# Spreading a weight quantisation over three engines in an attention and feed-forward kernel, with GpSimd taking q's parts ahead of k's

## The reference

```python
xn = layernorm(x)
# attention: 16 query heads and 4 key/value heads, 8 features each, causal
q = rope((xn @ Wqa @ Wqb).reshape(b, s, 16, 8))
k, v = split((xn @ Wkva @ Wkvb).reshape(b, s, 4, 8, 2)); k = rope(k)
attn = softmax(causal(q @ k.T * 8 ** -0.5)) @ v @ Wout + bout
# feed-forward, fp4 linear: both operands are quantised and dequantised
def fp4_quant_dequant(x):          # per block of 16
    scale = max(max(abs(xb)) / 6, 1e-12)
    return grid(abs(xb / scale)) * sign(xb) * scale
gate, up = fp4_linear(xn, w_gate), fp4_linear(xn, w_up)      # 128 -> 352
ffn = fp4_linear(silu(gate) * up, w_down)                    # 352 -> 128
out = x + attn + ffn
```

## Time and profile before

| | us |
|---|---|
| median of 3 runs | 919.4 |
| lowest, highest | 917.61, 923.97 |
| the profiled execution: time | 914.5 |
| the profiled execution: span of the core | 912.7 |
| TensorE busy | 765.5 (84%) |
| VectorE, GpSimd, ScalarE busy | 643.7, 593.8, 568.4 |
| mean granted TensorE clock | 0.989 |

### The profile page before, as it was taken

The page is one execution under the profiler, slowest core; times in us unless marked ns, Lnnn a source line. Parts: engine busy times, 40 slices in busy tenths (PEclk is TensorE's granted clock), DMA queues, the critical chain, the costliest instruction groups (busy, mean ns, idle before and its releaser), DMA issues.

```text
span 912.7 us, 22388 instructions
## 1 busy us (share of the span) xinstructions
PE 765.5 (84%) x6769; PEld 486.9 (53%) x6861; DVE 643.7 (71%) x1444; ACT 568.4 (62%) x1201; POOL 593.8 (65%) x688
## 2 busy tenths in 40 slices
PE   2376889898997989879897989979988998988786
PEld 1233555656564565646555565645656565655443
DVE  4789877787776877666776778758786877677501
ACT  1134677666757766665765667567666768576673
POOL 3446777678766767667676677656677777765541
PEclk9998999999999999989999999999999999999999
DMA  5314121323232122322312132221223222130000
GB/s 132 94 33 114 55 62 41 89 62 90 53 84 69 53 60 54 90 53 71 74 59 62 52 89 63 82 60 49 64 54 89 64 86 55 53 77 12 25 23 13
DMA packets 66279, 58.47 MB, mean 64 GB/s; under 512 B 17299, under 2 KB 56179, under 8 KB 66171
## 3 DMA queue, kind: packets, MB, share of 16 engines
q1 hardware_dynamic: 66170, 57.04, 23.4%
HBM read 31.81 MB, written 18.61 MB: 55 GB/s over the span
## 4 chain that ended last, share of the span: by engine, by line
PE 45%; ACT 15%; issue 15%; DVE 11%; POOL 6%; another core or an unknown queue 3%; SPq 2%; DMA 1%; DVEq 0%; ACTq 0%; POOLq 0%
PE pv_ps L1033 10%; PE exp_ps L1015 7%; ACT P L836 6%; PE max_ps L1000 5%; DVE neg_max L641 5%; PE misc_ps L1100 5%; PE misc_ps L1051 4%; POOL P L491 3%; PE misc_ps L1061 3%; PE max_ps L1001 2%; PE misc_ps L1069 2%; ACT oT L855 2%; ACT h_mag L946 2%; PE misc_ps L1098 2%
## 5 line engine op out<-in xcount | busy, mean ns | idle before, releaser
L641 DVE TENSOR_REDUCE neg_max<-max_ps 128x1 f32<-128x512 f32 (+3 forms) x768 | 430.9, 597 | 180.2 <-PE max_ps L1001 177.9
L836 ACT ACTIVATE P<-exp_ps 128x512 f32<-128x512 f32 x512 | 293.1, 604 | 197.7 <-PE exp_ps L1015 106.4
L1015 PE MATMUL exp_ps<-Q,K 128*128 128x128 bf16 (+3 forms) x932 | 210.8, 294 | 26.6 <-ACT P L836 22.6
L1000 PE MATMUL max_ps<-K,Q 128*128 128x384 bf16 (+2 forms) x768 | 198.9, 278 | 37.8 <-DVE neg_max L641 15.9
L1001 PE MATMUL max_ps<-Kd,Q 128*128 128x128 bf16 x1024 | 190.5, 221 | 1.0 <-DVE neg_max L641 0.8
L1033 PE MATMUL pv_ps<-P,V 128*32 128x512 f32 (+3 forms) x2048 | 165.3, 438 | 5.9 <-issue 2.6
L491 POOL TENSOR_SCALAR_AFFINE_SELECT P<-P 128x512 f32<-128x512 f32 x256 | 154.0, 638 | 19.2 <-ACT P L839 19.2
L1000 PEld LDWEIGHTS max_ps<-K,Q 128*128 128x128 bf16 x768 | 76.4, 100 | 112.3 <-DVE neg_max L641 47.7
L1001 PEld LDWEIGHTS max_ps<-Kd,Q 128*128 128x128 bf16 x1024 | 100.4, 99 | 36.9 <-issue 18.6
L1015 PEld LDWEIGHTS exp_ps<-Q,K 128*128 128x128 bf16 x1024 | 79.6, 98 | 71.9 <-ACT P L836 46.6
L839 ACT ACTIVATE P<-exp_ps 128x512 f32<-128x512 f32 x128 | 78.3, 612 | 36.8 <-PE exp_ps L1015 36.7
(11 more groups left out here) (112 smaller groups left out, 1084.1 us busy)
## 6 DMA issues: line engine op xcount, KB each, us to landing
Q<-q_scr SPq DMA_DIRECT2D x64, 224.0 KB
q_scr<-q_split SPq DMA_DIRECT2D x16, 384.0 KB, 2.6
Kd<-K SPq DMA_DIRECT2D x64, 96.0 KB
x_in<-x SPq DMA_DIRECT2D x16, 256.0 KB, 2.8
q_scr<-q_split SPq DMA_DIRECT2D x16, 256.0 KB, 2.9
x_res<-x SPq DMA_DIRECT2D x16, 256.0 KB, 5.2
out<-y SPq DMA_DIRECT2D x16, 256.0 KB, 4.4
K<-k_scr SPq DMA_DIRECT2D x64, 48.0 KB
```

What stands on the lines that cost most here:

```text
L641: nc.vector.tensor_reduce(neg_max[:, pr // 4, i, heads[0]:heads[0] + len(heads), pr % 4], max_ps[r % 3][:, 0:len(heads) * n].rearrange("p ...
L836: nc.scalar.activation(P[g % 2][:, hh + r % 2, col:col + 512], ps[:, :], ACT.Exp, scale=SCALE).then_inc(exp_done, 1)
L1000: nc.tensor.matmul(ps[:, col:col + d], Qt, Kt[:, half, g, 0:d], start=True, stop=True)
L1015: last = nc.tensor.matmul(exp_ps[n % 2][:, col:col + width], K[par][:, half, pr // 2, kb * 128:(kb + 1) * 128], Q[par][:, pr, kb * 128:S], ...
```

## The change

In all steps, GpSimd's work on the third batch ahead is reordered. Before: `k_rope`, `q_rest`, `k_rest`, `hidden(2)`, third part of q, third part of k. Now: `q_rest`, `k_rope`, third part of q, `k_rest`, `hidden(2)`, third part of k. ScalarE's order is as before. In the opening, GpSimd's wait for the loads moves from before step -2 to after it, and the quantisation of the weights is cut into pieces inside step -2: VectorE takes the largest magnitudes and scales ahead of `x_max`, GpSimd the multiplication by the inverse ahead of `xq`, ScalarE the multiplication by 2^22 ahead of `x_mag`, and VectorE the rest in two pieces, one after `q_sin` and one after `v_stage`. Only the copies of the transposed weights stay between the steps.

```diff
@@ GpSimd
-            pool.wait_ge(weights_in, 16 * N_WEIGHTS)
+            def scale_weights():
+                pool.wait_ge(w_step, 4)
+                nc.gpsimd.tensor_tensor(blocks(w_raw[:, :]), blocks(w_raw[:, :]), spread(w_inv[:, :]), ALU.mult).then_inc(w_step, 1)
...
+                    if T.t0 == FIRST_T:
+                        scale_weights()
                     T.wait(pool, x_scales, 4, 2, 4)
                     nc.gpsimd.tensor_tensor(blocks(xq[:, :]), blocks(xn[:, :, :].rearrange("p c e -> p (c e)")),
...
                 if T.has(2):
+                    T.wait(pool, q_casts, 2, 2, 1)
+                    nc.gpsimd.tensor_tensor(q_rest[:, :], q_rope[:, :], q_split[:, 0, :], ALU.subtract).then_inc(q_pool, 1)
                     T.wait(pool, k_muls, 2, 2, 2)
                     nc.gpsimd.tensor_tensor(k_rope[:, :], k_cos[:, :], k_sin[:, :], ALU.add).then_inc(k_pool, 1)
-                    T.wait(pool, q_casts, 2, 2, 1)
-                    nc.gpsimd.tensor_tensor(q_rest[:, :], q_rope[:, :], q_split[:, 0, :], ALU.subtract).then_inc(q_pool, 1)
+                    T.wait(pool, q_casts, 2, 2, 2)
+                    nc.gpsimd.tensor_tensor(q_split[:, 2, :], q_rest[:, :], q_split[:, 1, :], ALU.subtract).then_inc(q_pool, 1)
                     T.wait(pool, k_casts, 2, 2, 1)
                     nc.gpsimd.tensor_tensor(k_rest[:, :], k_rope[:, :], k_split[:, 0, :], ALU.subtract).then_inc(k_pool, 1)
                 hidden(T, 2)
                 if T.has(2):
-                    T.wait(pool, q_casts, 2, 2, 2)
-                    nc.gpsimd.tensor_tensor(q_split[:, 2, :], q_rest[:, :], q_split[:, 1, :], ALU.subtract).then_inc(q_pool, 1)
                     T.wait(pool, k_casts, 2, 2, 2)
                     nc.gpsimd.tensor_tensor(k_split[:, 2, :], k_rest[:, :], k_split[:, 1, :], ALU.subtract).then_inc(k_pool, 1)
...
-            iterate(pool, iteration)
+            iterate(pool, iteration, lambda: pool.wait_ge(weights_in, 16 * N_WEIGHTS))
@@ VectorE
+            def weight_scales():
+                dve.wait_ge(weights_in, 16 * N_WEIGHTS)
+                dve.wait_ge(consts_set, 2)
+                nc.vector.tensor_reduce(w_max[:, :], blocks(w_raw[:, :]), AX.X, ALU.max, apply_absolute_value=True).then_inc(w_step, 1)
+                scales(dve.wait_ge, w_max[:, :], w_scale[:, :], w_inv[:, :], w_step)
+
+            def weight_magnitudes():
+                dve.wait_ge(w_step, 6)
+                magnitudes(lambda s, n: dve.wait_ge(s, 6 + n), w_mag[:, :], w_step)
+                dve.wait_ge(w_step, 8)
+                nc.vector.tensor_tensor(w_raw[:, :], w_raw[:, :], w_mag[:, :], ALU.add).then_inc(w_step, 1)
+
+            def weight_values():
+                dve.wait_ge(w_step, 9)
+                nc.vector.tensor_tensor(w_raw[:, :], w_raw[:, :], w_mag[:, :], ALU.subtract).then_inc(w_step, 1)
...
+                if T.t0 == FIRST_T:
+                    weight_scales()
                 reduces(0, 2)
...
+                if T.t0 == FIRST_T:
+                    weight_magnitudes()
                 reduces(2, 3)
...
                 reduces(2, 5)
+                if T.t0 == FIRST_T:
+                    weight_values()
...
-            def quantize_weights():
...
-            iterate(dve, iteration, quantize_weights)
+            iterate(dve, iteration, store_weights)
@@ ScalarE
+                if (slot, r) == (1, 4) and T.t0 == FIRST_T:
+                    act.wait_ge(w_step, 5)
+                    nc.scalar.activation(w_mag[:, :], w_raw[:, :], ACT.Copy, scale=2.0 ** 22).then_inc(w_step, 1)
```

More of the change, by code:

```diff
@@ L629, in magnitudes, with store_weights @@
                 nc.vector.tensor_scalar(mag, mag, 1.5 * 2.0 ** 22, None, ALU.max).then_inc(sem_, 1)
+            def weight_scales():
[11 more added lines that the diff above has]
+                nc.vector.tensor_tensor(w_raw[:, :], w_raw[:, :], w_mag[:, :], ALU.subtract).then_inc(w_step, 1)
+                dve.wait_ge(w_step, 10)
+                nc.vector.tensor_tensor(blocks(w_raw[:, :]), blocks(w_raw[:, :]), spread(w_scale[:, :]), ALU.mult).then_inc(w_step, 1)
+            def store_weights():
+                dve.wait_ge(w_transposed, 1)
+                for n in range(2):
+                    nc.vector.tensor_copy(wguT[:, n, :], max_ps[n][:, 0:F]).then_inc(w_ready, 1)
+                for c, (_, cn) in enumerate(FC):
+                    nc.vector.tensor_copy(wdT[0:cn, c, :], exp_ps[0][0:cn, c * E:(c + 1) * E]).then_inc(w_ready, 1)
             def reduce_tile(T, pr, r):
@@ L788, in iteration @@
                 reduces(7, 3, 4, 5)
-            def quantize_weights():
-                dve.wait_ge(weights_in, 16 * N_WEIGHTS)
-                dve.wait_ge(consts_set, 2)
-                nc.vector.tensor_reduce(w_max[:, :], blocks(w_raw[:, :]), AX.X, ALU.max, apply_absolute_value=True).then_inc(w_step, 1)
-                scales(dve.wait_ge, w_max[:, :], w_scale[:, :], w_inv[:, :], w_step)
-                dve.wait_ge(w_step, 4)
-                nc.vector.tensor_tensor(blocks(w_raw[:, :]), blocks(w_raw[:, :]), spread(w_inv[:, :]), ALU.mult).then_inc(w_step, 1)
-                dve.wait_ge(w_step, 5)
-                nc.vector.tensor_scalar(w_mag[:, :], w_raw[:, :], 2.0 ** 22, None, ALU.mult).then_inc(w_step, 1)
-                dve.wait_ge(w_step, 6)
-                magnitudes(lambda s, n: dve.wait_ge(s, 6 + n), w_mag[:, :], w_step)
-                dve.wait_ge(w_step, 8)
-                nc.vector.tensor_tensor(w_raw[:, :], w_raw[:, :], w_mag[:, :], ALU.add).then_inc(w_step, 1)
-                dve.wait_ge(w_step, 9)
-                nc.vector.tensor_tensor(w_raw[:, :], w_raw[:, :], w_mag[:, :], ALU.subtract).then_inc(w_step, 1)
-                dve.wait_ge(w_step, 10)
-                nc.vector.tensor_tensor(blocks(w_raw[:, :]), blocks(w_raw[:, :]), spread(w_scale[:, :]), ALU.mult).then_inc(w_step, 1)
-                dve.wait_ge(w_transposed, 1)
-                for n in range(2):
-                    nc.vector.tensor_copy(wguT[:, n, :], max_ps[n][:, 0:F]).then_inc(w_ready, 1)
-                for c, (_, cn) in enumerate(FC):
-                    nc.vector.tensor_copy(wdT[0:cn, c, :], exp_ps[0][0:cn, c * E:(c + 1) * E]).then_inc(w_ready, 1)
             for k in (K[0], K[1], Kd):
```

## The result

| | before | after |
|---|---|---|
| median, runs of one session | 921.68 us (4 runs, 917.61 to 924.6) | 937.51 us (4 runs, 936.0 to 939.9) |
| after : before | | 1.0195 [1.0157, 1.0232], or +18.0 us [14.5, 21.4] |
| profiled execution: time, span | 914.5, 912.7 | 938.8, 937.1 |

The change makes the kernel slower by 2%. The time is 4.5 us above the forecast of 933 and inside its range; as a difference, +14.1 was forecast and +18.0 measured. (The us are the ratio's; the two medians lie 15.8 apart.) The profiled execution of before is faster than its fastest timed run, so the two traces differ by 24.4 us where the times differ by 18.0. Positions far into the span are therefore not compared; single steps are.

A forecast was written before the change was run, and what follows sets the result against it. TensorE, busy 84% of the span, was taken as the bound; other engines' delays count only where it waits. Steps cost 18.4 us, the opening gains 4.3: 919.4 + 14.1 = 933.5, said as 933, range 922 to 939.

The forecast's parts named there:

- The order's mechanism: Loop steps T = 0 to 13: late `k_rope` stalls ScalarE 0.75 us; `causal` and the weighted sums come 1.37 us later.
- The stall's second path: Loop step: TensorE's exponential tiles wait for stalled ScalarE, 0.75 to 1.0 us, overlapping the 1.37 and not added.
- rival "half": Loop: TensorE or ScalarE makes up part of the delay, leaving 14 x 0.7 - 4.3 = +5.5, 925 us; chance 0.13.
- slack at 426.1 or `k_rope` in time: Condition of the rival that the loop step absorbs the delay and only the opening counts: 915.1 us; chance 0.10.
- 4.3 us gained: Opening: earlier variance and new order start q's third part 4.6 us earlier; gain taken as 4.3, ends 2.8 and 4.6.
- Products of q come 3.7 earlier, too late to be held up by this: Opening: VectorE's wait for loads until 12.54 and weight scales until 16.0 don't delay q's products.
- It is hidden by 0.5: Opening: VectorE's weight piece after `q_sin` is done by 21.5, before `k_cos` is due at 22.0.
- The rival "the opening loses its gain": Opening: VectorE's and GpSimd's weight operations hold each other up, k 1.5 to 1.8 later, gain 2.8, 935 us; chance 0.10.

The follow-up runs named there:

- the two direct runs: After with before's GpSimd order in every step except step -2: 919.52 us, ratio 1.0002; after with before's GpSimd order in all steps: 923.02 us, ratio 1.0008.

## Why the prediction was right or wrong

**The order's mechanism was right, step by step.** Forecast in T = 6: `causal` 425.08 - 418.14 = 6.94 after `q_rest`, the weighted sums 9.39 after it. Measured: 6.91 and 9.36. Forecast stall of ScalarE: 0.75. Measured: the cast is 0.79 later and 0.66 of it is idle time. Forecast growth of the wait for `causal`: to 0.4 or more, in the trace 0.45.

**Its size was a little low.** 1.35 per step was forecast and 1.47 measured; the order by itself costs 20.5 us by the times instead of 18.4. The two moves taken apart cost 0.66 and 0.74. The prediction's working, for each alone, gives 0.63 for q's third part (without the stall the cast ends at 421.34, and 0.18 + 1.13 + 0.41 + 0.9 brings k's third part to 423.96 instead of 423.33) and 0.75 for the stall, 1.38 together, like the 1.37 of the forecast. The weighted sums come 1.34 later after `q_rest`; the other 0.13 of the 1.47 lies between them and the next `q_rest` and was not traced to an instruction.

**The stall's second path was judged rightly as parallel.** The forecast said that TensorE is also held up through the exponential tiles, and that this overlaps with the late `causal`. With `causal` in time the stall costs 0.60, with `causal` late by as much 0.74: nothing like the sum of the two is paid. (The times of these two kernels, +8.0 and +4.4 us, don't rank them this way, and their intervals overlap.) The rival "half" (14 x 0.7) is thus what happens when only `causal` is relieved, and that kernel gave +8.0. Neither rival's condition, slack at 426.1 or `k_rope` in time, was met in the changed kernel.

**The opening was wrong.** The step that failed is the term "4.3 us gained". The changed kernel with before's order in the loop, where only the opening is left, measured +0.2 us [-2.7, +2.9]: nothing gained. Two links of its working failed.

The first is "Products of q come 3.7 earlier, too late to be held up by this", about VectorE's new wait for the loads and the scales of the weights. It held only in after's trace, with the last load landed before 12.28. In the four other traces of such openings the chain starts at that landing, and `q_sin` is 0.6 to 2.5 later. The prediction reckoned with the one landing of before's trace, and not with a longer `x_scale`, which took 1.58 for 0.18.

The second is "It is hidden by 0.5", about VectorE's piece after `q_sin`. The prediction asked whether VectorE would reach `k_cos` in time. In after's trace it was in time (22.04, just behind TensorE's end at 21.96), but GpSimd was not: it stood behind VectorE's addition and subtraction, 0.78 in `q_rest` and 1.07 in `k_rope`. The third part of q came 3.05 earlier instead of 4.6, the first maxima 3.1.

The rival "the opening loses its gain" had the first link of this: it let VectorE wait for GpSimd's `q_rope`, and one operation on `w_mag` did, for 0.95. Without that, by my estimate, the addition would have ended at 21.2, when `q_rest` started at 21.20. It had the rest the wrong way round, since the time was then lost on GpSimd. Its gain of 2.8 is above what the two direct runs show (+0.2 and, with the old order, +0.7 [-1.0, +2.5]); the whole change against the order only gives 2.5, from two ratios with intervals of 3.5 us each way, so 2.8 is unlikely and not excluded.

The rule quoted in the prediction, from the Trainium skill, "SBUF — State Buffer", section "Who interferes with whom", says that whoever issues first has the shared ports for its whole instruction; these rows agree. The prediction weighed it for one pair and one victim, and I should have gone through every pair of the stretch in both directions. The section also names VectorE's `tensor_scalar` among the operations that can contend with GpSimd, and `x_scale` (32 columns), issued at 15.31 beside GpSimd's 2.10 us multiplication from 14.77, took 1.58 where it took 0.18 in before's trace; the trace agrees.

**The later wait was undersized in the other direction.** By itself it is worth 4.0 us [1.4, 6.4] in the times. It had been counted as one gain with the spreading of the weights, and the two have opposite signs. The quantisation between the steps was hidden behind the DRAM trip in before (the earlier trace rows against the end of the earlier trace rows), and in the kernel with the wait's move alone the chain still runs over the Kd copy. So spreading it could gain nothing there, and it cost some 4.7, give or take 3.

**How the sum came out near all the same.** The order was 2.1 too low, the opening 4.5 to 5.0 too favourable. Both errors point the same way, and together they would give +20.7 to +21.2; +18.0 [14.5, 21.4] was measured against the forecast of +14.1. The sum came out near because the order, by far the larger term, was nearly right, and because this measurement lies below what the parts add up to, within its interval. The last is luck.

**Open.** Whether step -1 takes back a part of a head start: the stretch from the first maxima to `q_rope` of T = 0 varies by more than 5 us between the traces, with the granted clock, and moving the half clock elsewhere changed nothing that was measured. Why the kernel with `k_rope` behind `q_rest` alone is faster than its steps say.

## What to carry to other kernels

On an engine that works strictly in order, putting an instruction behind a wait for another engine makes all its readers wait too; before moving one, list who needs it and when, and look whether the idle time that it filled was free. Work that is hidden behind a transfer costs nothing where it is: spreading it into gaps of busier stretches can only gain if its end is awaited, and it can collide there with the chain that counts. Moving a wait from one engine's queue to another's takes it off the chain only if nothing of the chain stands behind it there; look at the latest time that the awaited event can come, and not at one trace. When a change has two parts, cost them apart: here the moved wait was worth 4 us by itself, and the rest of the change lost it again and more.

## What the runs showed of the hardware that I had not expected

- **VectorE and GpSimd held each other up in both directions, and small operations paid the most for their size.** GpSimd's 128x512 subtraction took 1.94 and 2.23 for 1.16, its 128x128 operations 1.50 to 1.53 for 0.42 to 0.46 beside VectorE's 1120-wide ones, and a VectorE operation of 32 columns 1.58 for 0.18 beside GpSimd's multiplication.
- **The same 11 loads landed at different times.** The work behind the last load started at 12.62 in before's trace, and at 13.29, 13.77, 14.30 and 15.05 in four other kernels that wait for the loads at the same place. An order that is tuned to one landing time is tuned to one execution.
- **At the four turns of the hardware loop TensorE has a gap of 2.9 to 4.5 us** in both traces: 3.27, 4.26, 2.86, 4.24 before, 4.50, 3.17, 4.18, 4.30 after. This is why step lengths were compared inside a turn.
